# Down weights unpacked in the last stage, whose first round goes by pairs of chunks over all eight PSUM banks

## What is computed

```python
def dequantize(W_q, scale, zero):
    hi, lo = W_q >> 4 & 15, W_q & 15
    w = jnp.stack([hi, lo], axis=-1).reshape(out, half * 2)
    w = (w.reshape(out, -1, 64) - zero[:, :, None]) * scale[:, :, None]
    return w.reshape(out, half * 2)
g = jnp.einsum('bsh,ih->bsi', x, Wg)
u = jnp.einsum('bsh,ih->bsi', x, Wu)
h = jax.nn.silu(g) * u
return jnp.einsum('bsi,hi->bsh', h, Wd)
# x = x + layernorm(ffn(layernorm(x)))
```

## Time and profile before

| | us |
|---|---|
| median of 3 runs | 2848.43 (2848.03 to 2848.68) |
| time of the profiled run | 2843.23 |
| its span, first to last instruction | 2841.5 |
| PE busy in the span | 2719.2 (96%) |
| DVE, ACT, POOL busy | 1256.9, 888.1, 1057.6 |
| all packets of the DMA queues | 21.2% of 16 engines' span |

### The profile page before, as it was taken

One profiled execution on the slowest core, in us unless ns is written; L12 is line 12 of the kernel. 1 busy time (PEld: TensorE's weight loads), 2 busy tenths in 40 slices (PEclk: granted clock), 3 DMA queues, 4 the chain that ended last, 5 costly groups with the idle time before them and its releaser, 6 DMA issues. The chain is left out here.

```text
span 2841.5 us, 42146 instructions
## 1 busy us (share of the span) xinstructions
PE 2719.2 (96%) x17472; PEld 1154.8 (41%) x17472; DVE 1256.9 (44%) x1595; ACT 888.1 (31%) x1591; POOL 1057.6 (37%) x586
## 2 busy tenths in 40 slices
PE   6999899999999999989959999999999998999998
PEld 3445433333333333224424444444444443444443
DVE  6333777878778777525642333332233320010001
ACT  3211466666666666630011111111111110000000
POOL 0000377777777777842222233323223320010001
PEclk9999999999999999999979999999999999999999
DMA  4223101101011010022222232232223223223220
GB/s 170 78 76 90 29 16 42 32 16 29 28 32 29 17 29 2 1 82 105 103 76 80 82 93 80 76 90 80 80 82 93 80 72 118 70 85 123 69 69 30
DMA packets 200761, 187.15 MB, mean 66 GB/s; under 512 B 22416, under 2 KB 175504, under 8 KB 200592
## 3 DMA queue, kind: packets, MB, share of 16 engines
q1 hardware_dynamic: 200592, 184.76, 21.2%
HBM read 134.74 MB, written 49.81 MB: 65 GB/s over the span
## 5 line engine op out<-in xcount | busy, mean ns | idle before, releaser
L728 POOL TENSOR_TENSOR c_prob<-c_prob 128x1024 f32<-128x1024 f32 (+1 forms) x288 | 605.0, 2120 | 515.2 <-ACT c_prob L626 512.7
L642 DVE TENSOR_REDUCE c_maxes<-c_s 128x2 f32<-128x1024 f32 (+3 forms) x640 | 645.8, 1058 | 194.7 <-PE c_s L482 194.7
L626 ACT ACTIVATE c_prob<-c_s 128x512 f32<-128x512 f32 (+1 forms) x1152 | 597.9, 571 | 299.3 <-PE c_s L504 185.3
L504 PE MATMUL c_s<-c_q,c_k 97*128 97x512 f16 (+3 forms) x1280 | 366.7, 352 | 10.1 <-ACT c_prob L626 1.7
L1179 POOL TENSOR_TENSOR e_hl<-e_h,e_hh 128x512 f16<-128x512 f32 (+1 forms) x88 | 120.8, 1373 | 491.8 <-ACT e_hh L1150 491.8
L519 PE MATMUL c_ctx<-c_prob,v_sb 128*32 128x512 f32 (+3 forms) x2560 | 293.4, 539 | 0.2 <-ACT c_c L615 0.2
L1070 PE MATMUL e_gp<-x_hi,e_w_hi 128*128 128x512 f16 x704 | 267.8, 380 | 20.8 <-DVE e_w_lo L1102 20.8
L1123 DVE SCALAR_TENSOR_TENSOR e_h<-e_up,e_silu 128x512 f32<-128x512 f32 x84 | 58.1, 692 | 493.3 <-PE e_up L1072 493.3
L1071 PE MATMUL e_gp<-x_lo,e_w_hi 128*128 128x512 f16 x704 | 267.8, 380 | 0.0
L1072 PE MATMUL e_gp<-x_hi,e_w_lo 128*128 128x512 f16 x704 | 267.6, 380 | 0.0
L1070 PE MATMUL e_up<-x_hi,e_w_hi 128*128 128x512 f16 x672 | 254.7, 379 | 0.0
(11 more groups left out here) (134 smaller groups left out, 3072.2 us busy)
## 6 DMA issues: line engine op xcount, KB each, us to landing
h_hi<-e_hh SPq DMA_DIRECT2D x84, 128.0 KB, 1.8
h_lo<-e_hl SPq DMA_DIRECT2D x84, 128.0 KB, 1.8
f_h_hi<-h_hi SPq DMA_DIRECT2D x7, 1344.0 KB, 8.5
f_h_lo<-h_lo SPq DMA_DIRECT2D x7, 1344.0 KB, 6.9
b_x<-L_attn_x SPq DMA_DIRECT2D x16, 512.0 KB, 6.6
c_q<-qk_hi SPq DMA_DIRECT2D x64, 128.0 KB, 3.1
d_x<-L_attn_x SPq DMA_DIRECT2D x16, 512.0 KB, 4.9
x_dram<-d_x SPq DMA_DIRECT2D x16, 512.0 KB, 2.6
```

What stands on the lines that cost most here:

```text
L504: last = nc.tensor.matmul(S2[:, h % 2, at:at + w], K[:, g % 2, k * P:(k + 1) * P], Q[:, g % 2, b, h, q:q + w], start=True, stop=not diag)
L626: nc.scalar.activation(prob(g, s, 0, w)[:, h, :], S2[:, h % 2, 0:w], ACT.Exp, scale=exp_scale).then_inc(exp_done, 1)
L642: last = nc.vector.tensor_reduce(MAXES[:, g % 2, t // TPB, heads, t % TPB, u], S1[:, heads, at:at + w], AX.X, ALU.max)
L728: return nc.gpsimd.tensor_tensor(one, one, two, ALU.add)
```

## The change

Stage E keeps only the gate and up tasks: gate of chunk c + 1 beside (c, 0), up of c + 1 beside (c, 2). The 24 down tasks move into stage F with their buffers and semaphores, and run there back to back: SP loads them all in order (210 DMAs), DVE unpacks k + 1 and then cuts k, POOL scales, ACT cuts. ACT issues the loads of h and x for both blocks of the first round, 18 DMAs, ahead of its first cut. PE's first round no longer goes product by product. For each of the first 16 tasks (8 pairs of chunks by 2 halves) it waits for the cut of that task and then runs its 24 matmuls over all four (u, s), so that all eight banks accumulate; then it waits for the last of the 24 tasks, and finishes the four products one after another with chunks 16 to 21. The later rounds are as they were.

```diff
-    for c in range(FULL - 1):
-        put(c, 0, (DOWN, c // 2, c % 2))
-        put(c, 1, (GATE, c + 1, 0))
+    for c in range(FULL):
+        put(c, 0, (GATE, c + 1))
         if c + 1 < FULL:
-            put(c, 2, (UP, c + 1, 0))
...
+    tasks = [(m, half) for m in range(WORD_PAIRS + 2) for half in range(2)]
+    APART = 8
...
+    parts = [(0, 2), (2, 8), (8, FULL)]
...
+            def load_words(k):
+                slot, (m, half) = k % 2, tasks[k]
+                cols = slice(half * BANK, (half + 1) * BANK)
+                if k >= 2:
+                    sp.wait_ge(scaled, k - 1)
+                for first, n, row in loads(tasks[k]):
+                    sp.dma_start(RAW[first:first + n, slot, :], words[row:row + n, cols]).then_inc(raw_loaded[slot], 16)
+                    for r in range(n // RUN):
+                        part = slice(first + r * RUN, first + (r + 1) * RUN)
+                        g = row // RUN + r
+                        for table, dst in ((zeros, ZEROS), (scales, SCALES)):
+                            sp.dma_start(dst[part, slot, :], table[g:g + 1, cols].broadcast_to([RUN, BANK])
+                                         ).then_inc(raw_loaded[slot], 16)
...
-            load_first()
-            load(0, 1)
+            for k in range(len(tasks)):
+                load_words(k)
...
+            def first_round():
+                for k, (m, half) in enumerate(tasks[:2 * APART]):
+                    if half == 0:
+                        arrived(2 * m)
+                    pe.wait_ge(cut_lo, k + 1)
+                    for u in range(2):
+                        for s in range(2):
+                            for c in chunks_of(m):
+                                part_product(u, s, c, [half])
+                pe.wait_ge(cut_lo, len(tasks))
+                for u in range(2):
+                    for s in range(2):
+                        for c in range(2 * APART, CHUNKS):
+                            last = part_product(u, s, c, range(2))
+                        last.then_inc(product, 1)
...
         def _(dve):
+            def unpack(k):
...
+                if k:
+                    dve.wait_ge(shifted, k)
+                dve.wait_ge(raw_loaded[slot], loaded_by(k))
...
+                if k >= 2:
+                    dve.wait_ge(cut_lo, k - 1)
...
+            dve.wait_ge(cleared, 1)
+            unpack(0)
+            for k in range(len(tasks)):
+                if k + 1 < len(tasks):
+                    unpack(k + 1)
+                cut(k)
...
         def _(act):
+            for i, (first, end) in enumerate(parts):
+                for u in range(2):
+                    for buf, src in ((H_HI, h_hi), (H_LO, h_lo)):
+                        act.dma_start(buf[:, u, first:end, :], src[first * P:end * P, rows(0, u)]
+                                      .rearrange("(c p) t -> p c t", p=P)).then_inc(part_loaded[i], 16)
...
+            for u in range(2):
+                act.dma_start(X[:, u], x1_dram[rows(0, u), :].rearrange("(s p) d -> p s d", p=P)
+                              ).then_inc(x_loaded[u], 16)
+            act.wait_ge(cleared, 1)
+            for k, task in enumerate(tasks):
+                n, planes = shape(task)
+                act.wait_ge(scaled, k + 1)
+                nc.scalar.activation(target(task, wd_hi), W[0:n, k % 2, 0:planes, :], ACT.Copy, scale=WS
+                                     ).then_inc(cut_hi, 1)
...
         def _(pool):
...
+            for k, task in enumerate(tasks):
+                n, planes = shape(task)
+                w = W[0:n, k % 2, 0:planes, :]
+                pool.wait_ge(shifted, k + 1)
+                nc.gpsimd.tensor_tensor(w, w, SCALES[0:n, k % 2, :].unsqueeze(1).broadcast_to([n, planes, BANK]), ALU.mult
+                                        ).then_inc(scaled, 1)
```

More of the change, by code:

```diff
@@ L909, in _, with gate_and_up @@
                 residual(i, False)
[L912 removed]
+def gate_and_up(nc, x2_hi, x2_lo, quantised, h_hi, h_lo, sem):
     KC, T = x2_hi.shape[1], x2_hi.shape[2]
@@ L933, in put @@
         tasks.append(task)
[L934 to L936 removed]
+    for c in range(FULL):
+        put(c, 0, (GATE, c + 1))
         if c + 1 < FULL:
[L938 to L972 removed]
+            put(c, 2, (UP, c + 1))
+    ready = {c: max(m for m, t in enumerate(tasks) if t[1] == c) + 1 for c in range(CHUNKS)}
+    def loads(task):
+        kind, at = task
         if at == FULL:
[L974 to L977 removed]
+            return [(slice(of * REST, (of + 1) * REST), of, slice(FULL * P, inter)) for of in (GATE, UP)]
+        return [(slice(0, P), kind, slice(at * P, (at + 1) * P))]
+    copies = [len(loads(t)) * (1 + 2 * P // RUN) for t in tasks]
     def loaded_by(m):
@@ L1002, in height, with target @@
             return REST if c == FULL else P
[L1004 to L1012, removed]
+        def target(task, w):
+            kind, at = task
+            return w[:, kind, at % 2]
         @block.sync
@@ L1019, in load @@
                     sp.wait_ge(scaled, m - 1)
-                for first, n, row, into, kind, cols in loads(tasks[m]):
+                for into, kind, cols in loads(tasks[m]):
                     words, scales, zeros = quantised[kind]
[L1022 to L1030, removed]
-                        for table, dst in ((zeros, ZEROS), (scales, SCALES)):
[L1032 to L1040, removed]
@@ L1077, in unpack @@
             def unpack(m):
-                task, slot = tasks[m], m % 2
-                n, planes = shape(task)
+                slot = m % 2
                 if m:
@@ L1262, in _, with part_product @@
-            block_product(0, 0, True)
-            block_product(0, 1, True)
+            def part_product(u, s, c, halves):
+                hh, hl = (h[:, u, c, s * P:(s + 1) * P] for h in (H_HI, H_LO))
+                for stat, w, a, z in ((hh, wd_hi, 1, 0), (hh, wd_lo, 0, 0), (hl, wd_hi, 0, 1)):
+                    for n in halves:
+                        last = nc.tensor.matmul(YP[:, u, s, n * BANK:(n + 1) * BANK], stat, w[:, c, n * BANK:(n + 1) * BANK],
+                                                start=(c == 0 and a == 1), stop=(c == CHUNKS - 1 and z == 1))
+                return last
```

158 lines of the change are left out of this document (98 added, 60 removed).

## The result

The changed kernel takes 2920.77 us (median of 4 runs, 2919.85 to 2921.70), the kernel before, on the same chips, 2848.23 us (2847.01 to 2848.68). The ratio is 1.0259, with a 95% interval of 1.0246 to 1.0271: slower by 72.5 us, where 64 was forecast (2912.4, range 2893 to 2931). The profiled run took 2919.85 us, its span is 2918.1.

What follows compares the result with a forecast made beforehand. PE sets the end, so only its waits count: ACT free at 25 us, 122 to the last cut, 39.4 to round 1, less 122.4 before, gives +64 us on 2848.4: 2912.4 us, range 2893 to 2931.

Steps and rivals of the forecast that it cites:

- Part 1: Stage E without the 24 down tasks: PE is not waiting for them, gain between 0 and 1.8 us, taken as 0.
- The length of a task: Load loop of two slots in F: a cycle of 11.48 us for two tasks, 5.74 each; bounds 10.57 to 12.0.
- rows 6: Profile rows of stage E's first task in the kernel before: the undisturbed load loop, DVE beginning 6.04 us after load start.
- A: Time after S at which ACT is free for its first cut: taken as 25 us, between 8.3 and 31.
- Rival 3: In F, SP's issues are the only limit and slots never wait: +22 us, chance 0.05.
- When the pipeline starts: Start of F: ACT's 18 issues of h and x delay its first cut to 25 us; PE begins about 2.4 later.
- Rival 1: Start of F: ACT is not held by its issues, +48 to +52 us; chance 0.13 together with POOL not slowed.
- Sum to R: R, the last down cut's time after S, is A + 122 us, between A + 114 and A + 128.
- After round 0: Ahead of round 1 in F: PE waits 6.7 us for h's reload, as products end 7.8 us apart, not 28.5.
- rows 3: Profile rows of stage F's products before: 28.50 us each, the first 30.15, so PE's return from idle costs 1.65.
- S: Start of block F, where SP issues its first load: 2364.28 us in the kernel before.
- Rivals 2, 4 and 5: Respectively: queues hold up each other's issues, +72 to +85, 0.14; clock stays low, about +110, 0.04; stage E gains, not slower, 0.02.

Runs made afterwards that it cites:

- run 2: Kernel before, down tasks kept in stage E, only F's first round going pair by pair with h and x loaded by ACT: 2855.9 us, ratio 1.0032.
- run 5: Changed kernel with four load slots instead of two for words, zeros and scales: 2913.9 us, ratio 1.0242.
- run 10: Changed kernel with four load slots, h in pieces of two chunks behind every second cut, and 20 tasks by pairs instead of 16: 2884.8 us, ratio 1.0136.
- run 4: Changed kernel with only h chunks 0 and 1 issued ahead of ACT's first cut, the other 14 DMAs between cuts 0 to 4: 2921.0 us, ratio 1.0259.
- run 9: Changed kernel with h beyond chunk 1, and x, loaded only behind ACT's last cut, a probe of the preparation: span 2983.5 us in a single execution.

## Why the prediction was right

The mechanism was right: the load loop sets the pace, ACT's issues hold the first cut back, and the last cut gates the rest of the round and then the reload of h. The sizes were near, in part by luck, and nearly all of the small misses fell on the same side.

*Part 1, nothing won in stage E*: 893.47 against 893.50 us. Right, and run 2 has the reverse: with the tasks back in E the time is back, but for the order's 8 us.

*The length of a task*: 5.74 us forecast, 5.75 measured; POOL's scale is 3.26 us wherever DVE's cut stands beside it. That it came out to 0.01 is in part luck: the usual load takes 5.7 us, not the 6.04 of rows 6, some take 6.8 to 7.1, and the two differences nearly cancel. The range had been drawn from the two tasks of rows 6 alone; its upper end, a cycle of 12.0, gives A + 126 by the prediction's own eight cycles, not the A + 128 that it states. What I missed is that a second limit lies right behind: without the load loop the pace is 5.29, not the 3.6 of DVE alone, as run 5 shows. "DVE is not the limit, nor is POOL" was true of each and not of both, for they exclude each other (below). Rival 3, with SP's issues at 4.1 us a task as the only limit, was for that reason not possible: its +22 us would have needed a pace that run 10 does not reach even with loads ahead.

*When the pipeline starts*: A = 25 was mis-sized; it measured 29.2, within the bounds of 20.5 to 31. The prediction let SP's first four tasks add half of their 8.5 us to the 20.5; all of it would give 29.0, an estimate that the measured value fits, as does the longer A of run 5, where six tasks' loads lie in that time. The mechanism as told, ACT held by its issues, is what the trace of the changed kernel shows. But run 4 shows that its 29 us are not saved by freeing ACT: the first cut comes 17 us sooner and the last one 1.5, since the tasks' loads then land later. Taking h and x out of the way altogether is worth 12 to 15 us (run 9). Rival 1 (+48 to +52 if ACT isn't held) would have failed on this: in run 4 ACT makes its first cut at 12.2 us, and the time is still 73 us above the kernel before.

*Sum to R*: R less A 122 forecast, 123.6 measured, the small tasks included. The hole ahead of the last cut was forecast at 31 and is 32.5.

*After round 0*: the wait for h 6.7 forecast, 7.0 measured, and 6.9 again in run 2. The one term that was left out is behind it: PE's clock falls in that hole as well (0.50 in the first 4 us of round 1), and round 1 to the end takes 2.4 us more. The return that was counted, behind the last cut, cost 2.1 (33.2 us for 144 matmuls) and not the 1.65 of rows 3: there the clock was back sooner, with 12 matmuls in the first 4 us at a mean of 0.60 against 10 at 0.50 in round 1 here.

The ledger of the 76.6 us between the two spans: 70.5 from S to round 1, 2.4 behind it, -0.2 in stage E, and 3.9 ahead of stage E, where the code is the same. The last is not the change's: in ten profiles here whose code is the same up to that point, the first matmul of E lies at 1467.2 to 1470.0 in nine and at 1464.8 in run 5, which has the changed kernel's stage E; it is at 1464.9 in the profile of before, whose run was 5 us under the median of its kernel. So 72.7 remain, against 72.5 by the medians. Of the 8.7 that the forecast is short, 4.2 are A's, 1.6 the loop's with its small tasks, 0.7 lie between R and round 1 (0.4 the clock's first return, 0.3 the wait for h), and 2.4 are the second return of the clock; stage E gives 0.2 back.

*Rivals 2, 4 and 5*: SP's first eighteen issues lie 0.4 to 0.8 us apart, the last at 2376.50, and are not held up by ACT's: that one took 0.42 us inside an issue of ACT's of 6.55. The Trainium skill's sentence (Perfetto Trace Analysis, DMA Instruction — HWDGE) on a generator locked for one DMA at a time did not show as a hold of SP here: none of its first 36 issues took more than 0.69 us, while ACT's took up to 6.55. That the measured +72.5 is the time rival 2 names is chance: by that rival load 2 was to start at about 29 us, and it started at 15.1. The clock stayed up between tasks (0.97 over the 16 tasks, its start included). Nothing was gained in stage E.

## What to carry to other kernels

Preparation cost nothing here beside PE in stage E. Where PE has to wait for it, its price is its own pace, which one undisturbed loop of the trace gave nearly enough, less what PE can do meanwhile; ask what the last prepared piece gates. Ask also, of two engines that are each below the limit, whether they can run at the same time. Reordering a round so that its products end close together leaves the reload of the next operand less work to hide behind. When a queue is found held by its transfers, moving the issues away need not help: here it changed nothing until the loads could run ahead.

## What the runs showed of the hardware

DVE and POOL exclude each other in both directions here. POOL's 128x1024 multiply takes 2.34 us with DVE idle (at 2380.73 in the changed kernel) and 3.26 where DVE's two-input cut of 1.22 us had begun just before; and DVE's `tensor_scalar` of 0.42 us takes 2.57 where POOL had begun before it:

```profile
2401.48 1.22 DVE L1310 SCALAR_TENSOR_TENSOR f_wd_lo<-f_w,f_wd_hi 128x1024 f16<-128x1024 f32 x1
2402.61 2.57 DVE L1296 TENSOR_SCALAR f_nibbles<-f_raw 128x512 int32<-128x512 int32 x1
...
2401.64 3.26 POOL L1364 TENSOR_TENSOR f_w<-f_w,f_scales 128x1024 f32<-128x1024 f32 x1 [14.27 <-DVE f_w L1302]
```

The unpack ends at 2405.18, when POOL's scale ends at 2404.90. That makes a step of 5.29 us out of 3.26 and 2.0. By the rule of the Trainium skill (SBUF — State Buffer, Who interferes with whom: whoever issues first holds the shared port, and a `tensor_scalar` may enter a mode that needs it), the trace agrees on both sides. I had applied it to POOL only.

A load whose tables came as two broadcasts of 256 KB, four table rows each, was there some 3 us later than one with eight broadcasts of 64 KB on the same queue (8.8 against 5.7 us from the first issue). And 7.5 MB of h and x cost 12 to 15 us of a loop of two slots, which by itself keeps the DMA engines busy 47% of the time, whether they came in 29 us or over 130; with four slots and h in pieces they did not slow the loop (run 10).

PE's clock had fallen after a hole of 7 us: the granted clock was 0.50 over the first 4 us of round 1, and the round's first 57 us held 11 matmuls fewer, which is 2.4 us.
